# A chunked delta-rule recurrence on one core: stages of the finished chunk and gate operations at other levels of the round

## The reference

```python
def step(carry, inp):
    s, mem = carry
    mem = DECAY * mem + sdt
    hard = (mem > THR)
    spike = ...                                   # value of hard
    mem = mem - spike * THR
    alpha = sigmoid(abt + alpha_spike * spike)
    beta = sigmoid(bbt[..., None] + sum(spike * beta_spike))
    active = (sum(hard) > 0)
    alpha = where(active > 0, alpha, 1)
    beta = beta * active
    s = s * alpha[..., None]
    u = einsum('bhd,bhdv->bhv', kt, s)
    s = s - beta[..., None] * einsum('bhd,bhv->bhdv', kt, u)
    s = s + beta[..., None] * einsum('bhd,bhv->bhdv', kt, vt)
    out = einsum('bhdv,bhd->bhv', s, qt)
    return ((s, mem), out)
```

## Time and profile before

| | us |
|---|---|
| median of 3 runs | 1451.66 |
| lowest, highest | 1448.28, 1468.2 |
| the profiled execution | 1459.68 (span 1457.9) |

### The profile page before, as it was taken

One profiled execution on the slowest core, in us unless ns is written; L12 is line 12 of the kernel. 1 busy time (PEld: TensorE's weight loads), 2 busy tenths in 40 slices (PEclk: granted clock), 3 DMA queues, 4 the chain that ended last, 5 costly groups with the idle time before them and its releaser, 6 DMA issues. The chain is left out here.

```text
span 1457.9 us, 41117 instructions
## 1 busy us (share of the span) xinstructions
PE 1191.8 (82%) x17200; PEld 835.2 (57%) x17200; DVE 740.0 (51%) x2398; ACT 482.9 (33%) x1327; POOL 296.0 (20%) x582
## 2 busy tenths in 40 slices
PE   1698755888988898898899888587897798789778
PEld 1122123777777787787788877246445544744554
DVE  4756626777767777777766453126124213512421
ACT  2444301233333333333344333144224324422532
POOL 4100022223323322322333331202001100200110
PEclk9799955899989998999999789787898799789879
DMA  2000000000000000000000000300000000000000
GB/s 72 0 1 0 1 0 1 3 4 4 3 3 4 3 3 3 3 3 3 4 4 4 4 3 3 119 8 0 1 15 0 0 0 14 0 0 14 0 0 7
DMA packets 11733, 11.40 MB, mean 8 GB/s; under 512 B 1532, under 2 KB 9840, under 8 KB 11568
## 3 DMA queue, kind: packets, MB, share of 16 engines
q1 hardware_dynamic: 11567, 9.01, 2.0%
HBM read 7.96 MB, written 1.05 MB: 6 GB/s over the span
## 5 line engine op out<-in xcount | busy, mean ns | idle before, releaser
L628 POOL TENSOR_TENSOR work<-work 128x128 f32<-128x128 f32 x160 | 72.4, 452 | 379.0 <-PE banks L820 363.7
L820 PE MATMUL banks<-work 64*64 64x64 f32 x3072 | 108.5, 243 | 13.1 <-DVE gates L701 9.9
L309 DVE SCALAR_TENSOR_TENSOR mom<-gates 128x16 f32<-128x16 f32 x512 | 111.5, 218 | 9.8
L305 DVE SCALAR_TENSOR_TENSOR gates<-mom,gates 128x16 f32<-128x16 f32 x512 | 107.7, 210 | 12.5 <-ACT gates L396 6.9
L850 PE MATMUL banks<-work,gates 64*64 64x32 f32 x2560 | 110.8, 226 | 2.0 <-issue 1.1
L870 PE MATMUL banks<-work 64*64 64x32 f32 x2560 | 110.1, 227 | 0.0
L706 DVE TENSOR_TENSOR work<-work,banks 128x128 f32<-128x128 f32 x128 | 36.6, 286 | 136.5 <-PE banks L860 136.2
L850 PEld LDWEIGHTS banks<-work,gates 64*64 64x64 f32 x2560 | 97.0, 143 | 14.4 <-issue 11.2
L870 PEld LDWEIGHTS banks<-work 64*64 64x64 f32 x2560 | 101.4, 148 | 0.2
L701 DVE COPY_PREDICATED gates<-work,banks 128x256 f32<-128x256 uint32 x192 | 100.8, 525 | 1.1
L860 PEld LDWEIGHTS banks<-work 64*64 64x64 f32 x2048 | 83.5, 150 | 19.7 <-issue 18.3
(11 more groups left out here) (225 smaller groups left out, 2411.2 us busy)
## 6 DMA issues: line engine op xcount, KB each, us to landing
work<-in_x_dram SPq DMA_DIRECT2D x5, 256.0 KB, 2.8
out_dram<-work SPq DMA_DIRECT2D x4, 256.0 KB, 2.3
gates<-in_w_ff_dram SPq DMA_DIRECT2D x3, 256.0 KB, 4.6
wv_sb<-in_wv_dram SPq DMA_DIRECT2D x1, 512.0 KB, 4.7
work<-in_w_out_dram SPq DMA_DIRECT2D x1, 512.0 KB, 4.0
gates<-in_x_Wq_dram SPq DMA_DIRECT2D x1, 512.0 KB, 6.5
gates<-in_x_Wk_dram SPq DMA_DIRECT2D x1, 512.0 KB, 7.2
gates<-in_x_Wv_dram SPq DMA_DIRECT2D x1, 512.0 KB, 8.2
```

The costliest lines, as they stand in the source:

```text
L305: ve.scalar_tensor_tensor(mem[:, :, t], neg_mem, -0.9, mem[:, :, t], ALU.mult, ALU.add).then_inc(charged, 1)
L309: ve.scalar_tensor_tensor(neg_mem, mem[:, :, t], 1.0, mem[:, :, t], ALU.is_gt, ALU.subtract)\
L628: gp.tensor_tensor(first, first, by, ALU.mult).then_inc(ks_ok, 1)
L820: last = pe.matmul(level_out(l)[to, a], KS[rows, n.two, hp], late[rows, hp], start=True, stop=True)
```

## The change

The stages move between the levels of the loop. Nothing is computed otherwise. On PE `turn_ks(nxt)` goes from level 1 to 2, `spike_sums(gate)` from the end of level 2 to its middle, `values`, `correct` and `turn_out` from 2 to 3, `solve` from 3 to 4, `write_state` from 4 to 5, and both halves of `read_state` and `read_chunk` to behind the loop, around `turn_start(aft)`. On DVE `spikes` and `update` stay first, `prefix` and `keep` go ahead of `add_xt`, and `scale_key`, `scale_query` and `alpha` go one level down. On ACT the squares leave the end of the chunk's own round for levels 1 and 2 of the next, where `normalise`, `keep_res`, `keep_u`, `keep_out`, `soft_alpha` and `start_xt` also come one level or two later. On POOL `root` goes from the end of the chunk's own round to between `suffix` 2 and 3 of the next, and `keys`, `products` stand apart with `suffix(aft, 4)` between. The suffix products stay on POOL and wait for `tot_ok` also. `scale_key` waits for `o_old` in place of `s_mm`, since the reads of the state now come later.

```diff
                 def suffix(n, l):
                     first = first_half(KS[:, n.two], l)
+                    gp.wait_ge(lvl_mm, n.it * LEVELS + l + 1)
...
-                    gp.wait_ge(lvl_mm, n.it * LEVELS + l + 1)
...
                         gp.wait_ge(ks_ok, n.it * NKS + l)
+                        gp.wait_ge(tot_ok, n.it * NTOT + l)
...
                     if aft:
                         suffix(aft, 1)
                         suffix(aft, 2)
+                    if prev:
+                        root(prev)
+                    if aft:
                         suffix(aft, 3)
                     if aft2:
                         keys(aft2)
+                    if aft:
+                        suffix(aft, 4)
+                    if aft2:
                         products(aft2)
                     if aft:
-                        suffix(aft, 4)
                         suffix(aft, 5)
                     if aft2:
                         suffix(aft2, 0)
-                    if cur:
-                        root(cur)
...
                     if n.it >= 4:
-                        ve.wait_ge(s_mm, n.it - 3)
+                        ve.wait_ge(o_old, n.it - 3)
...
+                    if gate:
+                        spikes(gate)
+                    if prev:
+                        update(prev)
                     for l in range(1, NINV + 1):
                         h = 6 * (l - 1)
-                        if l == 1 and gate:
-                            spikes(gate)
-                        if l == 1 and prev:
-                            update(prev)
                         spike(scan, h)
                         if nxt and l < NINV:
                             add_x(nxt, l)
                         spike(scan, h + 1)
-                        if nxt and l < NINV:
-                            add_xt(nxt, l)
-                        spike(scan, h + 2)
                         if aft:
                             prefix(aft, l)
+                        spike(scan, h + 2)
                         spike(scan, h + 3)
                         if aft:
                             keep(aft, l)
-                        if nxt and l == NINV:
+                        spike(scan, h + 4)
+                        if nxt:
                             add_xt(nxt, l)
-                        spike(scan, h + 4)
                         spike(scan, h + 5)
                         if l == 1 and gate_old:
                             beta(gate_old)
+                        if l == 2 and aft2:
+                            scale_key(aft2)
                         if l == 3 and gate:
                             drive(gate)
-                        if l == 1 and aft2:
-                            scale_key(aft2)
-                        if l == 2 and aft2:
+                        if l == 3 and aft2:
                             scale_query(aft2)
-                        if l == 4 and gate:
+                        if l == 5 and gate:
                             alpha(gate)
...
                         if l == 1 and gate_old:
                             beta_sums(gate_old)
-                        if l == 1 and nxt:
+                        if l == 2 and nxt:
                             turn_ks(nxt)
+                        if l == 2 and gate:
+                            spike_sums(gate)
                         if cur:
-                            if l == 2:
+                            if l == 3:
                                 values(cur)
-                            if l == 3:
+                            if l == 4:
                                 solve(cur)
-                            if l == 4:
-                                read_state(cur, 0)
+                            if l == 5:
                                 write_state(cur)
-                            if l == 5:
-                                read_chunk(cur)
...
-                        if l == 2 and cur:
+                        if l == 3 and cur:
                             correct(cur)
-                        if l == 2 and prev:
+                        if l == 3 and prev:
                             turn_out(prev)
-                        if l == 2 and gate:
-                            spike_sums(gate)
-                        if l == 4 and cur:
-                            read_state(cur, 1)
+                    if cur:
+                        read_state(cur, 0)
                     if aft:
                         turn_start(aft)
+                    if cur:
+                        read_state(cur, 1)
+                        read_chunk(cur)
                     if aft2:
                         level(aft2, 0)
...
-                        if l == 1 and nxt:
+                        if l == 1 and prev:
+                            square(prev, 0)
+                            square(prev, 1)
+                        if l == 2 and nxt:
                             keep_ks(nxt)
-                        if l == 1 and prev:
+                        if l == 2 and prev:
+                            square(prev, 2)
+                            square(prev, 3)
+                        if l == 3 and prev:
                             normalise(prev)
-                        if cur and l == 2:
+                        if l == 3 and cur:
                             keep_res(cur)
```

35 lines of the change are left out of this document (13 added, 22 removed).

## The result

The changed kernel is slower: its median is 1514.32 us (1510.45 to 1517.29, four runs), and that of the kernel before beside it 1450.07 (1448.28 to 1468.2, four runs). The ratio is 1.0412, with a 95% interval from 1.0325 to 1.0499. The forecast was 1408 us, and neither its range (1376 to 1438) nor its slower rival (1475 to 1503) holds the time. The profiled execution took 1513.36 us.

What follows compares the result with a forecast made beforehand. TensorE's waits were taken to set the round, with its lowered clock the second cost. 22 × (0.8 + 0.9) + 9 × (0.4 + 0.3) = 43.7 us off: 1416 against the profiled execution, 1408 against the median; range 1376 to 1438.

Steps and rivals of the forecast that it cites:

- slower rival: `beta` comes too late on VectorE, so the wait before `spike_sums` grows: 1475 to 1503 us, chance 0.06.
- Where the waits go: Early in the round: `turn_ks` stops waiting; about 0.75 us before `make_z(nxt, 2)` and about 1.0 before `spike_sums`.
- `root` costs nothing: `root(prev)` between GpSimd's suffixes: 3.2 us before `turn_out(prev)`, covered by 3.8 us of TensorE work.
- The clock: TensorE's clock in the loop: 0.9 us back per round with the scan, 0.3 per late round.
- the argument that no single wait would be above 1.1: Upper bound of the clock's gain: all 1.85 us back, since a round with a wait of 1.30 kept full clock.
- The lower bound of the clock's term: Nothing of the 1.85 us comes back, if three waits of 1.94 us within 4 us count like one of 1.75.
- the split wait keeps the clock down: Rival: the clock gives nothing back; only 0.8 and 0.4 us a round remain, 21 us, 1431 us, chance 0.25.
- The full-clock round: A round with the scan at full clock: 6.04 + (16.25 − 4.10) + 0.3 = 18.5 us, 0.8 less.
- 6.04, with 6.3 as the upper end: Microseconds from the round's first matmul group to the end of `beta`, counted from VectorE's queue; `spike_sums` waits for it.
- that 0.3: End of round: `read_chunk` waits uncovered for `read_state(cur, 1)`, priced at one matmul's length, 0.3 us (bounds 0 and 0.46).
- The wait of `level(aft, 4)`: It goes, as `prefix` and `keep` ahead of `add_xt` take 0.3 to 0.8 us off the level-to-level chain.
- Late rounds: The nine rounds after the scan: 0.4 us less at full clock and 0.3 from the clock each, 6.3 us together.

## Why the prediction was wrong

**Where the waits go: right.** `turn_ks` waits no more. `make_z(nxt, 2)` waits 0.55 us (said: 0.75) for VectorE's `add_x`, `spike_sums` 1.07 (said: 1.0) for `beta`. No wait came at `turn_out` or `solve`, `root` costs nothing, and the wait of `level(aft2, 0)` is gone. The stages outside the loop are unchanged.

**The clock: wrong, in sign and size, and this is the larger part of the miss.** The sum had a full-clock round of 18.5 and 0.95 of the 1.85 us still lost. The round of 23.74 less the full-clock 20.05 gives 3.7 lost (4.1 by the rounds with the wait filled). So the clock gave back −1.85 where +0.9 was said, 2.75 us in each of 22 rounds, 60 us. The step that failed is the argument that no single wait would be above 1.1 while a round with a wait of 1.30 had kept its clock. It took the longest single wait for what decides, from rounds of another make-up. The rows at hand spoke against it: the same wait of 1.75 stands ahead of the full-clock round at 510.66 (L839 0.46 us) and ahead of the slow one at 529.93 (0.71). Filling 1.1 us of waiting moved 83 us, and the kernel with waits of 0.55 and 0.6 (`spike_sums` late) has a falling clock too.

**The lower bound of the clock's term was none.** "Nothing comes back" is the loss of before, of about 1.85 a round. The bound was taken to be that a clock that falls costs what it cost before. But 1.85 was read as the cost in each round, and it is a mean. Of the 20 rounds of the kernel before from 294.39 to 721.02 us, six keep the clock and take 19.3 to 19.5 us, three take 20.9 to 21.1, and eleven take 22.3 to 23.1 and have a slow piece like this one, in the window of which the clock is 0.50:

```profile
529.96:536.79 6.83, 6.83 (x122) 5.63 (x124) 3.13 (x14) 1.69 (x6) 0.46 (x1) 0.50 0.01 2
```

So a fallen clock cost about 3 us there, in part of the rounds. In the changed kernel it falls in 19 of 20, and the slow piece is 10.10 us: about 4 us in nearly every round. The change made the falls more frequent and each one longer. `values` is not the difference: it lies in the slow piece in the kernel before as well (1.97 us at 406.08). I had laid out what TensorE does until `spike_sums`, and not what it does behind it. The rival "the split wait keeps the clock down" had the mechanism and priced it at the old loss, 1431 us. With a loss of 3.7 for 1.85 and the full-clock round of 18.5 it would have been 1431 + 22 × 1.85 = 1472.

The Trainium skill's section "A second HAM failure mode: psum-queue depth-cycling" ("TensorE: Matmul & The Clock Gate") says that small idle times between groups make the clock swing. The trace after agrees (0.80 behind waits of 0.55 and 1.07), and by this rule alone the change was one to distrust.

**The full-clock round: wrong by 1.55 us, another 34 us.** It came out at 20.05 instead of 18.5. That is one round; by the rounds with the wait filled (19.62) the miss is 1.1 us, and the 0.4 between them belongs to the clock's 4.1. The two together, 4.3 us, are the same either way. There are two terms. From L814 to `spike_sums` it is 6.80 us in the full-clock round and 6.41 in the next and in most others, said: 6.04, with 6.3 as the upper end. The chain from the start of `update` (L720) to the end of `beta` (L748) is as laid out: 502.28 + 0.42 − 499.31 = 3.39, and 521.94 + 0.42 − 518.97 = 3.39 in the next round, for 6.04 − 2.73 = 3.31. But `update` starts 3.27 and 2.88 behind L814 instead of 2.73, because `prefix(aft2, 0)` (L688), which waits for `level(aft2, 0)`, starts 1.29 and 0.91 behind the first L814, where it was 0.76 in the kernel before. `level(aft2, 0)` now follows `read_chunk` at once (its first matmuls start ahead of the last two of `read_chunk`), where it had a wait ahead of it in the earlier trace rows; and in the one full-clock round its L819 group takes 0.86 us at 496.43 for 0.45 elsewhere, which stays unexplained. TensorE starts 0.14 after `beta`, for which I had no term. From `spike_sums` to the next L814 it is 13.25, where 16.25 − 4.10 + 0.3 = 12.45 was said. A wait of 0.3 before a `level` is still in the round, and `read_state`, `turn_start`, `read_state`, `read_chunk` back to back cost about 0.8 where 0.3 was the price, if the rest of the difference is put down to them; the step that spread them took 0.6 off the mean round, with that wait. The bounds of that 0.3, up to 0.46, came from the length of a group and not from a row in which a matmul waits for a product just begun.

**The wait of `level(aft, 4)`: gone as said, and another came for it.** The wait of 0.30 at 537.14 in the timeline above stands behind `write_state`, in level 5: it is `level(aft, 5)` that waits. Before, half of `read_state` and `read_chunk` stood between `level(aft, 4)` and `level(aft, 5)`; the change took them from there to the end of the round, and there is no `make_x` in level 5. I had asked what `prefix` and `keep` gain and not what TensorE has left to cover them. They also run slower than I took them. `prefix` now starts at the same moment as `suffix` on GpSimd in most levels. From the timeline after:

```profile
507.65 0.42 DVE L688 TENSOR_TENSOR work<-work 128x256 f32<-128x256 f32 x1
507.68 0.66 POOL L626 TENSOR_TENSOR work<-work 128x128 f32<-128x128 f32 x1 [0.85 <-PE banks L819]
507.99 0.40 DVE L305 SCALAR_TENSOR_TENSOR gates<-mom,gates 128x16 f32<-128x16 f32 x1
...
508.42 0.65 DVE L309 SCALAR_TENSOR_TENSOR mom<-gates 128x16 f32<-128x16 f32 x1
...
535.57 0.42 DVE L688 TENSOR_TENSOR work<-work 128x256 f32<-128x256 f32 x1
...
536.57 0.42 DVE L702 COPY_PREDICATED gates<-work,banks 128x256 f32<-128x256 uint32 x1
```

The scan's two instructions take 0.40 and 0.65 us for 0.18 and 0.19 in the earlier trace rows, while GpSimd runs `suffix` and, from 508.30 to 509.03, `keys` (L594). Ahead of `level(aft, 5)` it is 1.00 us from the start of `prefix` to that of `keep`, for which the earlier trace rows has 0.43 (512.59 to 513.02) with one instruction of the scan between instead of two. I had used VectorE's distances as they stood where the two engines did not meet.

**Late rounds.** 18.31 us for 18.41, said: 17.7; 0.6 × 9 = 5 us. Here too the clock has a part: three of the eight have a clock of 0.82 to 0.91 and take 19.3 to 19.9 us, the others 16.5 to 18.0. What makes these longer than said was not taken apart.

Together: 22 × (2.75 + 1.55) + 5 = 100 us above the 1416 forecast for the profiled execution, 1516; it took 1513.36.

**What stays open.** What decides whether the clock falls behind a wait: the same wait of 1.75 us takes it down in 14 of 20 rounds of the kernel before and leaves it in six. What brings it back after 10.10 us in the changed kernel, after 6.72 with idle matmuls elsewhere and 6.83 in the kernel before; why VectorE's old order let more rounds keep it; and why most slow rounds of the changed kernel fall on 23.8 to 24.1 us. The clock figures of each kernel are from one profiled execution.

## What to carry to other kernels

A shorter wait is not a cheaper one as long as the clock falls behind it: first ask what the clock does, by putting idle matmuls over the whole array into the wait. If the time drops by more than the wait is long (83 us for 20 waits of 1.07 here), the clock is what is paid for. Price a fallen clock by the rounds in which it can fall and the length of a slow piece, not by the mean that it cost before the move. And before a consumer is moved to a later place, see what stands ahead of its producer: moving `beta` and `update` on VectorE, and `turn_ks` behind them, gave more than the change had taken away (1406.87 for 1514.32 us), and spreading two reads another 29, of which about 17 are seen in the rounds.

## What was not expected of the hardware

Waits of 0.55 and 1.07 us with two groups of small matmuls between took TensorE's granted clock to 0.50 for 10.10 us, in which it was busy all the time; two idle matmuls of 128x256, 1.1 us in a round of 19.6, kept it at 1.00 for 390 us. The same two in another level brought it from 0.79 to 0.89 and no further.

GpSimd and VectorE slow each other down when their float32 products of two SBUF inputs meet: `suffix` (128x128) takes 656 ns in the mean beside `prefix` and 428 otherwise, a 128x16 instruction of VectorE 0.18 us alone and up to 0.65 beside GpSimd. The Trainium skill ("GPSIMD Engine Reference", section "8. Key points") says that GpSimd shares its SBUF interfaces with VectorE and contends with instructions with two SBUF inputs; the trace agrees.
